# Causal attention on one Trainium2 core: the key-major queries from an addition on VectorE instead of a second stacking on TensorE

## The reference, cut to what matters

```
h = _layernorm(x, axis=-1) * (1 + ca) + sa
q = (x @ Wq.T).reshape(B, S, N_HEADS, HEAD_DIM).transpose(0, 2, 1, 3)
k = (x @ Wk.T).reshape(B, S, N_HEADS, HEAD_DIM).transpose(0, 2, 1, 3)
...
q, k = _apply_rope(q, k, cos, sin)
scores = jnp.einsum('bhqd,bhkd->bhqk', q, k) / math.sqrt(HEAD_DIM)
mask = jnp.triu(jnp.full((S, S), -jnp.inf, dtype=scores.dtype), k=1)
scores = scores + mask[None, None]
probs = jax.nn.softmax(scores, axis=-1)
out = jnp.einsum('bhqk,bhkd->bhqd', probs, v)
...
x = x + ga * _L0_attn_ref(h, L0_attn_Wq, L0_attn_Wk, L0_attn_Wv, L0_attn_Wo)
h = _layernorm(x, axis=-1) * (1 + cb) + sb
x = x + gb * _L0_ffn_ref(h, ...)
```

## Time and profile before

| what | us |
|---|---|
| median of 3 runs | 3744.88 (3739.05 to 3750.31) |
| the profiled execution | 3750.11 |
| its span, first to last instruction | 3748.0 |
| causal half, from the start to about | 590 |
| the other two parts | 3158 |

### The profile page before, as it was taken

How to read it: one execution, slowest core, us unless ns; L and a number is a source line. 1 busy time by engine, 2 the same in 40 slices (tenths; PEclk the granted TensorE clock), 3 DMA queues, 4 the chain that set the end, 5 groups by cost and what they waited for, 6 DMA issues and landing times. The chain is left out here.

```text
span 3748.0 us, 147316 instructions
## 1 busy us (share of the span) xinstructions
PE 3597.6 (96%) x64322; PEld 2745.5 (73%) x64322; DVE 3149.5 (84%) x4991; ACT 2410.4 (64%) x3791; POOL 2310.4 (62%) x1367
## 2 busy tenths in 40 slices
PE   6999995999999999999999999999999999999996
PEld 4777773777777777777777777777777777777774
DVE  5767664998889999988899998889999988899993
ACT  4555553666667676666676766667676766676663
POOL 1110104777677777776777777777777777677771
PEclk9999997999999999999999999999999999999998
DMA  1000001222222222222122222222222112221122
GB/s 58 4 4 7 4 7 49 58 55 57 55 57 59 65 53 58 52 61 61 52 57 56 55 62 60 55 57 55 64 61 58 52 52 53 56 57 53 52 53 70
DMA packets 122997, 188.78 MB, mean 50 GB/s; under 512 B 25054, under 2 KB 44278, under 8 KB 122108
## 3 DMA queue, kind: packets, MB, share of 16 engines
q1 hardware_dynamic: 122364, 179.36, 17.7%
HBM read 24.08 MB, written 4.19 MB: 8 GB/s over the span
## 5 line engine op out<-in xcount | busy, mean ns | idle before, releaser
L1319 POOL TENSOR_TENSOR rc<-rc,rnorm 128x1024 f32<-128x1024 f32 x384 | 731.2, 1904 | 392.8 <-DVE rnorm L170 375.7
L1313 POOL TENSOR_TENSOR rc<-rc,rs 128x1024 f32<-128x1024 f32 x384 | 910.9, 2372 | 7.2 <-DVE rs L1378 3.6
L1354 POOL TENSOR_TENSOR prob_b<-prob_b,rinv 128x1024 f32<-128x1024 f32 x192 | 365.2, 1902 | 361.0 <-DVE rinv L1459 361.0
L1372 DVE TENSOR_TENSOR rc<-proj,rope_b 128x1024 f32<-128x1024 f32 x384 | 465.8, 1213 | 86.0 <-ACT squares L1176 85.2
L1176 ACT ACTIVATE squares<-proj 128x1024 f32<-128x1024 f32 x384 | 392.9, 1023 | 179.5 <-PE proj L928 175.9
L1019 PEld LDWEIGHTS ring<-pT,vmoved 64*64 64x64 f32 x18432 | 378.8, 135 | 133.2 <-issue 133.1
L1378 DVE TENSOR_TENSOR rs<-proj,rope_b 128x1024 f32<-128x1024 f32 x384 | 466.3, 1214 | 0.0
L965 PEld LDWEIGHTS ring<-ident,rc 128*128 128x128 f32 x3072 | 361.6, 141 | 142.6 <-issue 44.9
L1386 DVE TENSOR_REDUCE sums<-squares 128x16 f32<-128x1024 f32 x384 | 464.1, 1209 | 0.0
L965 PE MATMUL ring<-ident,rc 128*128 128x128 f32 x3072 | 428.1, 277 | 15.3 <-POOL rc L1319 11.9
L1019 PE MATMUL ring<-pT,vmoved 64*64 64x32 f32 x18432 | 402.6, 220 | 22.4 <-issue 20.8
(11 more groups left out here) (173 smaller groups left out, 7906.6 us busy)
## 6 DMA issues: line engine op xcount, KB each, us to landing
vmoved<-vown SPq DMA_DIRECT2D x576, 128.0 KB
vmoved<-vown SPq DMA_DIRECT2D x192, 192.0 KB
vmoved<-vown SPq DMA_DIRECT2D x576, 64.0 KB
wqkv_raw<-in_L_ffn_Wqkv SPq DMA_DIRECT2D x40, 192.0 KB, 3.0
wo<-in_L_ffn_Wo SPq DMA_DIRECT2D x6, 512.0 KB, 5.2
x_attended<-xtok SPq DMA_DIRECT2D x8, 256.0 KB, 2.0
xtok_c<-x_attended SPq DMA_DIRECT2D x8, 256.0 KB, 4.5
out<-xtok_c SPq DMA_DIRECT2D x8, 256.0 KB, 2.8
```

The costliest lines, as they stand in the source:

```text
L1313: nc.gpsimd.tensor_tensor(rc[:, k % 2, c, :], rc[:, k % 2, c, :], rs[:, c, :], ALU.add).then_inc(add_done, 1)
L1319: nc.gpsimd.tensor_tensor(dst, dst, rnorm[:, k % 2, c * HEADS:(c + 1) * HEADS].rearrange("p (h o) -> p h o", o=1).broadcast_to([P, HEADS, ...
L1354: nc.gpsimd.tensor_tensor(pr, pr, rinv[:, :, :].rearrange("p q (s o) -> p q s o", o=1).broadcast_to([P, PAIRS, 2, KEYS]), ALU.mult).then_i ...
L1372: nc.vector.tensor_tensor(rc[:, k % 2, c, :].rearrange("p (h d) -> p h d", h=HEADS), proj[c][:, :].rearrange("p (h d) -> p h d", h=HEADS), ...
```

## The change

The second stacking (L392 and L393 of `stack_with_max`) is left out. PE fills the bank with the turned maxima alone; the maxima are held as fp32r and turned against the fp32r identity. VectorE adds this fill to qG, the row-major queries of the same group, and writes q2. ScalarE no longer reads this fill. Since qG is now read later, ScalarE's next copy into the same home of qG (there are two) waits until VectorE has made the addition of two groups before. VectorE makes the addition in the slot in which ScalarE made its copy: behind its key strips and in front of the turn, the norms and the maximum of that slot.

```diff
-BY_VECTOR = ("q", "qr", "k", "kr", "turn", "back", "yt")
+BY_VECTOR = ("q", "qr", "k", "kr", "stack2", "turn", "back", "yt")
...
-        negmax = sb("negmax", [P, 2, TILES, P])
+        negmax = sb("negmax", [P, 2, TILES, P], f32r)
...
-            def stack_with_max(gr):
+            def turn_max(gr):
                 bank = begin("stack2", gr)
-                stack(bank, gr, 0, False)
                 pe.wait_ge(max_d, PER * (gr + 1))
                 for j in range(TILES):
-                    last = nc.tensor.matmul(bank[:, j * P:(j + 1) * P], negmax[:, gr % 2, j, :], ident[:, :],
-                                            start=False, stop=(j == TILES - 1))
+                    last = nc.tensor.matmul(bank[:, j * P:(j + 1) * P], negmax[:, gr % 2, j, :], ident_r,
+                                            start=True, stop=True)
                 last.then_inc(g_fill, 1)
...
                 if i == 0:
-                    pe.wait_ge(g_act, GEN_ACT["stack2", gr] + 1)
+                    pe.wait_ge(g_dve, GEN_DVE["stack2", gr] + 1)
...
                     bank = filled("stackq", gr)
+                    if gr >= Q_HOMES:
+                        act.wait_ge(g_dve, GEN_DVE["stack2", gr - Q_HOMES] + 1)
                     nc.scalar.activation(qG[:, gr % Q_HOMES, :], bank[:, :], ACT.Copy).then_inc(g_act, 1)
...
-                gr = group_at(s, STACK2_AT + 1)
-                if gr is not None:
-                    bank = filled("stack2", gr)
-                    nc.scalar.activation(q2[:, gr % 2, :], bank[:, :], ACT.Copy).then_inc(g_act, 1)
...
-            nc.gpsimd.memset(negmax[:, :, :, :], 0.0).then_inc(clear_d, 1)
+            nc.gpsimd.memset(negmax[:, :, :, :].bitcast(f32), 0.0).then_inc(clear_d, 1)
...
+                gr = group_at(s, STACK2_AT + 1)
+                if gr is not None:
+                    bank = filled("stack2", gr)
+                    nc.vector.tensor_tensor(q2[:, gr % 2, :], bank[:, :], qG[:, gr % Q_HOMES, :].bitcast(f32), ALU.add).then_inc(g_dve, 1)
```

More of the change, by code:

```diff
@@ L474, in _ @@
                 if group_at(s, STACK2_AT) is not None:
-                    stack_with_max(group_at(s, STACK2_AT))
+                    turn_max(group_at(s, STACK2_AT))
                 gr = group_at(s, TURN_AT)
```

## The result

| | before | with the change |
|---|---|---|
| median, 7 runs each | 3745.79 us (3739.05 to 3750.87) | 3722.27 us (3717.92 to 3734.05) |
| ratio | | 0.9945, 95% interval 0.9928 to 0.9962 |
| the profiled execution, its span | 3748.0 us | 3730.8 us |

The kernel became faster by 0.55% (0.38 to 0.72%), some 21 us, and 3722 us lies 2 us from the forecast of 3724. A hit on the total says little about the steps, so each was checked in the trace.

The account below looks back on a forecast made before the run. PE was taken to bound the causal half, VectorE its 7 windows: 25 groups x 0.91 = 22.7 us, less 0.5 and 1.3, gives 21 us, so 3724 us against the 3744.9 median; range 3713 to 3735.

Parts of the forecast that it names:

- PE's saving: PE's load-to-load time at the second stacking and turned maxima falls from 1.35 to 0.44 us, 0.91 us a group.
- the pair: The two removed 512-column stacking matmuls, L392 and L393, taken as 0.34 us of PE time a group.
- the type: Four turned-maxima matmuls as fp32r instead of fp32: 0.44 us for 1.01, a gain of 0.57 a group.
- rival 3: 128-column fp32r matmuls take as long as fp32, so only 6.5 us is gained, 3738 us; chance 0.04.
- The addition: VectorE's add of turned maxima and row-major queries, replacing ScalarE's copy, taken as 0.60 us of queue time.
- Ordinary groups: Groups outside the 7 windows: the add ends 1.4 us after the scores, the turn starts at 2.17, no wait.
- the groups with a Newton step: Five groups behind windows, with the first layer norm's Newton step in front: 0.1 us wait each, 0.5 us lost.
- The windows: Seven groups where the second layer norm starts and VectorE bounds: five lose 0.27 us each, 1.3 in all; two count 0.
- the gap: VectorE's 0.33 us idle before the maximum at 286.90 in a window, taken as the only cover for the add.
- The full gain (1): The windows have unseen spare room, so all 32 groups gain 0.91 us: 29 us, 3716 us; chance 0.14.
- VectorE's lag in more groups (2): A longer add or late rden_w turn in ordinary groups halves the gain: about 10 us, 3735 us; chance 0.12.
- VectorE as the bound everywhere (4): The add holds up maxima and scores in every group: slower by 9 us, 3754, or 28, 3772; chance 0.04.

Follow-up runs that it names:

- run 1: The change with the maxima held and turned as fp32 again, VectorE's addition kept; 514.8 us from first score load to last exponential (505.4 with the change).
- run 2: The kernel before with only the maxima made fp32r, second stacking and ScalarE's copy kept; 511.2 us from first score load to last exponential (524.9 before).
- Run 3: The change without the addition: ScalarE copies the turned maxima alone, queries left out; 501.0 us from first score load to last exponential (505.4 with the change).
- run 4: The change with a second, equal VectorE addition into a spare tile; 513.1 us from first score load to last exponential (505.4 with the change).
- run 5: The change with layer norm h one slot later; 505.8 us from first score load to last exponential (505.4 with the change).

## Why the prediction was right, step by step

In the terms of the measure, the forecast was 21 us, and 19.5 were found.

- **PE's saving, 0.91 us a group: right**, 0.90 measured at each of the 31 fills between score loads, and 0.76 in the last group. Its split into 0.34 for the pair and 0.57 for the type was wrong: 0.46 and 0.45 (runs 1 and 2). The sum did not depend on it, but rival 3's price did: with no gain from the type, 10 us would have been left, not 6.5.
- **The addition, 0.60 us of queue: right**, by the difference of runs 3 and "with the change" (0.59) and by doubling it (0.59).
- **Ordinary groups have room: right.** Behind the first batch a second addition costs nothing in them, save for 0.23 us in the fifth group. The 0.5 us forecast for the groups with a Newton step was not there (0.16 us in the first batch, 0 in the five others). The 0.1 us taken for a semaphore there stood in no row; with the change, rden_w's load follows the end of the addition by 0.05 us in the window (278.50 to 278.55). Doubled, the addition costs 0.53 of its 0.60 us in these groups, so they had 0.07 us of room left.
- **The windows, +0.27 us each: nearly**, +0.18 in five; of the other two, taken as 0, one gained 0.16 and the other 0.33. That is 0.9 lost less 0.5 gained, where 1.3 had been forecast. The size was off by one reading: the gap was taken at its idle time of 0.33 us, while from start to start it is worth 0.42, and 0.60 - 0.42 = 0.18. The reason was incomplete too. The text held that VectorE bounds the window whatever PE saves, and spent the gap as cover for the addition alone. Runs 2 and 3 show that a window does profit from PE: without the addition it gains 0.41 us, of 0.45 and of 0.91 saved. The gap can close only once, so with the addition 0.59 is lost and 0.41 brought. PE's stops at the window's end are 0.80 + 0.35 = 1.15 us, as forecast (about 1.2), but the longer one stands in front of the turns of xn and not of the score load.
- **What the forecast did not have:** the wait of the next stacking. The short fill lets PE arrive earlier at L392, whose bank VectorE is still reading, for the projections times rope (L699) or for xtok (L735). In the trace this is the bank of the fill before the last, and the load comes right behind VectorE's reader, first in the first batch (the view shows the wait), then in the window (too short for the view to show one, 0.05 us from the reader's end to the load):

```profile
60.19 0.68 DVE L699 TENSOR_TENSOR rot<-gen,rope 128x512 f32<-128x512 f32 x1
...
60.92 0.19 PEld L392 LDWEIGHTS gen<-qk_hi,sel 128*128 128x128 f32 x1 [0.90 <-DVE rot L699]
```

```profile
275.62 0.68 DVE L735 TENSOR_TENSOR xtok<-gen,xtok 128x512 f32<-128x512 f32 x1
...
276.35 0.19 PEld L392 LDWEIGHTS gen<-qk_hi,sel 128*128 128x128 f32 x1
```

In later batches the same costs 0.21 us twice a batch. Outside the windows that is 0.85 in the first batch and 6 x 0.21 = 1.3 us after it, 2.1 us, the main part of what was missing. Run 3, which has no addition, has all of it. In runs 1 and 2, whose fill is longer, the 0.21 us are absent and the first batch loses 0.4 instead of 0.85.

The account: 24 x 0.90 + 0.76 = 22.4 us, less 2.1 us for this wait, 0.3 in the first batch, and 0.9 in the five windows, plus 0.5 from the two others, gives 19.6; measured 19.5. Part of the agreement with 21 is luck: against the 2.1 us that the forecast did not have stand some 1.4 us that it took off or left out for nothing (0.5 for the Newton groups, 0.4 in the five windows, 0.5 in the two others).

**The rivals.** The full gain (1) failed at the windows and at the banks. VectorE's lag in more groups (2) is what the 8.3 us of idle loads in front of rden_w's turn might have suggested, but there were 17.5 before the change, and run 4 shows the room. fp32r on 128 columns is not as slow as fp32 (3): 0.44 against 0.89 us. VectorE as the bound everywhere (4) would have needed more than a second addition of 0.6 us in each group.

The type was worth 0.45 us a group in run 2. The Trainium skill's four passes of true fp32 (FP8 and Floating Point Precision, TensorE Precision Notes) would have made it 0.64, by the estimate quoted ahead of the result. The trace agrees in part: the four fp32 matmuls are near that count, at 0.89 us, but the fp32r ones take 0.44 us and not a quarter of it.

## What to carry to other kernels

Price a matmul in a stream from load to load, and do not trust a cut between two kinds of matmul inside such a sum; the sum over the removed run was right to 0.01 us, its parts were off by 0.12. When a fill gets shorter, look at the next fill of every rotating bank: what PE now reaches earlier is still being read. A gap in an engine's queue can be closed from either side, by more work in front of it or by earlier input, but only once, so ask who it waits for before it is spent as cover, and measure it from start to start, as the work that is to fill it.

## What the runs showed that was not expected

The causal half repeats to a few hundredths of a microsecond (two profiles of the change: 505.42 and 505.39 us by the measure), while the rest, the same instructions in all kernels, does not: from the last exponential to the end it is 3748.0 - 569.3 = 3178.7 us before, 3745.2 - 559.6 = 3185.6 in run 1 and 3716.3 - 549.8 = 3166.5 in run 5. So single times are misleading here: run 1 took 3746.98 us beside 3745.31 for the kernel before, although its causal half was 10 us shorter, and run 5 took 3718.12 with one no shorter than that of the change. The granted clock goes with part of this scatter: it was 0.982 over the whole of run 1 and 0.986 in run 5, and among the seven runs of the change 0.983 in the slowest (3734.05 us) and 0.987 in the fastest (3717.92). It is not all of it, since runs of the kernel before took 3738.52 and 3750.62 us at the same 0.986. The cause stays open. The measure itself begins at the lower clock, both before and with the change: the granted clock reads 0.50 from 44 to 47 us and 1.00 from 60 us on.
